# Second attention of an audio tower on Trainium2: order of the softmax weights, the rows' turns and the low halves within a chunk

## The reference

```python
Q = (x @ Wq).reshape(B, T, h, k)        # 16 heads of 32
K, V = x @ Wk, x @ Wv                   # 4 heads of 32, each shared by four of Q's
Q = Q * cos + rotate_half(Q) * sin      # and K in the same way
scores = where(causal, Q @ K.T / sqrt(k), -inf)
A = softmax(scores)                     # within a sequence of 23 tokens
h = h + (A @ V) @ Wo                    # x is the layer norm of h
```

## Time and profile before

| | us |
|---|---|
| Median of 3 runs | 1508.97 |
| Lowest, highest | 1508.01, 1509.94 |
| The profiled execution | 1494.19 |
| its span | 1492.4 |
| PE busy | 1298.2 |
| DVE busy | 916.2 |
| ACT busy | 630.0 |
| POOL busy | 259.8 |
| Second attention, first projection to last product with V | 1142.2 to 1290.1 |

### The profile page before, as it was taken

One profiled execution on the slowest core, in us unless ns is written; L12 is line 12 of the kernel. 1 busy time (PEld: TensorE's weight loads), 2 busy tenths in 40 slices (PEclk: granted clock), 3 DMA queues, 4 the chain that ended last, 5 costly groups with the idle time before them and its releaser, 6 DMA issues.

```text
span 1492.4 us, 30422 instructions
## 1 busy us (share of the span) xinstructions
PE 1298.2 (87%) x10676; PEld 831.1 (56%) x10690; DVE 916.2 (61%) x1918; ACT 630.0 (42%) x1066; POOL 259.8 (17%) x304
## 2 busy tenths in 40 slices
PE   6878899999999999995857999999996778668997
PEld 3446677777777777773523444444543556424443
DVE  5776365555566556558782454555347765688886
ACT  3444444344444434441413444444533332236664
POOL 2444000000000000000003232233338510020000
PEclk9996999999999999997678999999998778789999
DMA  5121343435334353421404777776436620000000
GB/s 183 59 76 43 101 170 139 179 133 183 126 142 169 141 182 128 184 85 43 172 1 167 260 261 240 276 260 229 133 115 149 90 33 2 2 0 8 22 21 32
DMA packets 42703, 184.26 MB, mean 123 GB/s; under 512 B 8688, under 2 KB 9200, under 8 KB 34832
## 3 DMA queue, kind: packets, MB, share of 16 engines
q0 software_dynamic: 19744, 95.41, 19.4%
q1 hardware_dynamic: 19440, 75.41, 14.5%
q10 hardware_dynamic: 3456, 12.58, 2.4%
HBM read 135.65 MB, written 47.73 MB: 123 GB/s over the span
## 4 chain that ended last, share of the span: by engine, by line
PE 56%; DVE 18%; issue 14%; POOL 4%; ACT 4%; DMA 2%; DVEq 1%; ACTq 0%; POOLq 0%; SPq 0%
PE ps L919 14%; PE ps L920 14%; PE ps L921 14%; PE ps L1026 3%; PE ps L1009 3%; DVE ff L1991 2%; DVE amf L1998 1%; PE ps L1110 1%; POOL wide L512 1%; POOL rt_out L472 1%; PE ps L1042 1%; PE ps L1249 1%; POOL h L518 1%; PE ps L1342 1%; PE ps L1360 1%
## 5 line engine op out<-in xcount | busy, mean ns | idle before, releaser
L919 PE MATMUL ps<-nT_hi,wa_hi 128*128 128x368 f16 x448 | 147.2, 329 | 11.9 <-DVE wa_lo L1389 8.1
L920 PE MATMUL ps<-nT_lo,wa_hi 128*128 128x368 f16 x448 | 146.9, 328 | 0.0
L921 PE MATMUL ps<-nT_hi,wa_lo 128*128 128x368 f16 x448 | 146.3, 327 | 0.0
L1553 DVE TENSOR_TENSOR a<-sq,E 92x368 f32<-92x368 f32 x64 | 31.7, 535 | 136.2 <-ACT sq L690 136.2
L1725 DVE SCALAR_TENSOR_TENSOR nrm<-ps,xg,nrm 128x256 f32<-128x256 f32 x61 | 29.5, 483 | 133.7 <-ACT nrm L733 116.4
L502 POOL DMA_INDIRECT xg<-xrow,idx x61 | 61.0, 1001 | 276.9 <-PE ps L1110 121.9
L920 PE MATMUL ps<-wa_lo,nT_hi 128*92 128x128 f16 (+1 forms) x560 | 107.6, 236 | 0.0
L919 PE MATMUL ps<-wa_hi,nT_hi 128*92 128x128 f16 (+1 forms) x560 | 107.6, 236 | 0.0
L921 PE MATMUL ps<-wa_hi,nT_lo 128*92 128x128 f16 (+1 forms) x560 | 107.2, 236 | 0.0
L919 PE MATMUL ps<-wide,xT 128*128 x244 | 93.7, 384 | 13.2 <-issue 10.1
L702 ACT ACTIVATE yT_hi<-ps 128x368 f16<-128x368 f32 x64 | 27.9, 475 | 164.5 <-PE ps L1042 164.5
(11 more groups left out here) (308 smaller groups left out, 3354.5 us busy)
## 6 DMA issues: line engine op xcount, KB each, us to landing
we_st<-in_we POOLq DMA_DIRECT2D x16, 1536.0 KB, 6.8
wsp<-we_sp POOLq DMA_DIRECT2D x16, 1536.0 KB, 5.3
wide<-wsp SPq DMA_DIRECT2D x16, 1536.0 KB, 7.5
yslot<-yt POOLq DMA_DIRECT2D x61, 256.0 KB, 4.2
wq_st<-in_ffq SPq DMA_DIRECT2D x24, 512.0 KB, 6.1
wq_st<-in_ffq ACTq DMA_DIRECT2D x24, 512.0 KB, 4.4
wide<-in_wa SPq DMA_DIRECT2D x10, 1024.0 KB, 4.8
xt<-in_x SPq DMA_DIRECT2D x12, 512.0 KB, 3.4
```

The costliest lines, as they stand in the source:

```text
L919: nc.tensor.matmul(dst, lhs[0], rhs[0], start=start, stop=False)
L920: nc.tensor.matmul(dst, lhs[0], rhs[1], start=False, stop=False)
L921: return nc.tensor.matmul(dst, lhs[1], rhs[0], start=False, stop=stop)
L1553: V.tensor_tensor(B["a"][0:AT, j], B["sq"][0:AT, j], B["E"][0:AT, 2 * j:2 * j + 2].unsqueeze(2).broadcast_to([AT, 2, REP, AT]), ALU.mult). ...
```

## The change

Four orders and two waits are changed, all in the second attention. No operation is added or removed.

- DVE: `weights(c - 1)` stands between the root's request and `group_shift` in place of behind it. The three low halves of an inner chunk stand together behind `rotated`. `y_low(c - 1)` no longer stands at the end of chunk c, but behind rotate 0 and 1 of chunk c + 1 (the last one behind the loop).
- PE: the turn of the softmax weights stands right behind V, and the turns of all three row tiles behind it. It now waits only for the low half of the last tile of the group before. Each turn of a row tile gets a wait for ACT's move of the quarter of the softmax weights that lay in its bank.
- ACT: projection 4 is moved ahead of the normed tiles, and the quarters of the softmax weights are moved before the high halves of the rows.

```diff
@@ ScalarE
                 moved(c, 2)
                 moved(c, 3)
+                moved(c, 4)
                 if inner:
                     normed(k)
                     normed(k + 1)
-                moved(c, 4)
+                moved(c, 5)
+                if c:
+                    weights_turned(c - 1)
                 if inner:
                     high(k)
                     normed(k + 2)
-                moved(c, 5)
-                if inner:
                     high(k + 1)
                     high(k + 2)
-                if c:
-                    weights_turned(c - 1)
-                else:
+                if c == 0:
...
@@ TensorE
-            def turn(c):
+            def turn(c, k):
                 pe.wait_ge(f_s, c + 1)
-                pe.wait_ge(ln_lo, ready(2 * NT + min(NT, GT * (c + 3)) - 1))
+                pe.wait_ge(ln_lo, ready(2 * NT + k))
...
                 for j in range(2, 6):
                     project(c, j)
-                    if inner and j == 4:
-                        row_turn_l1(k)
+                if c:
+                    turn(c - 1, k - 1)
                 if inner:
-                    row_turn_l1(k + 1)
-                    row_turn_l1(k + 2)
-                if c:
-                    turn(c - 1)
+                    for j in range(k, k + GT):
+                        pe.wait_ge(f_pe, ready(4 * (c - 1) + 2 + j % 2))
+                        row_turn_l1(j)
                 scores(c)
...
-            turn(CH - 1)
+            turn(CH - 1, NT - 1)
@@ VectorE
                 rotate(c, 0)
                 rotate(c, 1)
+                if c > 1:
+                    y_low(c - 2)
                 if c:
                     if c + 1 < CH:
                         group_stats(c + 1)
+                    weights(c - 1)
+                    if c + 1 < CH:
                         group_shift(c + 1)
-                    weights(c - 1)
                 for j in range(2, 5):
                     rotate(c, j)
-                    if 0 < c < CH - 1:
-                        low(k + j - 2)
                 rotated(c)
+                if 0 < c < CH - 1:
+                    for j in range(GT):
+                        low(k + j)
...
                     centred(c)
-                    y_low(c - 1)
+            y_low(CH - 2)
```

## The result

| | before | changed |
|---|---|---|
| Median | 1508.59 us (4 runs) | 1493.83 us (4 runs) |
| Lowest, highest | 1508.01, 1509.94 | 1492.69, 1496.49 |
| The profiled execution | 1494.19 | 1496.49 |
| its span | 1492.4 | 1494.7 |

The ratio is 0.9903, with an interval from 0.9886 to 0.9921: 14.8 us faster, where 6.8 were forecast. The two profiled executions say something else again: the changed kernel's took 2.3 us longer. Both facts have to be explained.

What follows compares the result with a forecast made beforehand. The prediction took a ring between PE and DVE, each idle once a chunk, as the bound. Chunk terms +0.6 - 3.5 - 3.9 = -6.8 us, off the median 1508.97, gave 1502.2 us, range 1495.5 to 1507.

Steps and rivals of the forecast that it cites:

- The baseline: Whole execution: 14.8 us between profiled 1494.19 and median 1508.97 lie outside the changed work; the gain comes off the median.
- Theory A: Follow-up runs' expectation: only the second attention got faster, about 8 us; the rest of 14.8 us is stalls elsewhere.
- sign of being wrong: Behind the second attention: the prediction is wrong if the stage is shortened and the feed-forward part grows.
- The new wait at the third row's turn: Inner chunks, PE: the turn waits about 2 us for the first low half, now behind `qp`, with scores queued behind.
- The loss of 0.6 us: Chunk 1: scores end at 1202.5 against 1201.8, with turn, masks and scores priced at the low clock; +0.6 us.
- -3.5 forecast: Chunk 2: rotates ahead of `y_low` start statistics 3.5 us sooner; scores at the low clock; gain 3.5 us.
- the root's wait: Chunks 1 and 2: softmax weights no longer stand behind the root's result; 1.1 us of the root saved in chunk 2.
- -3.9 forecast: Chunk 3: rotates fill the wait for `y_high`, `qp` 3.3 us earlier, scores 0.6 us cheaper; gain 3.9 us.
- the price of the scores: Chunk 3: scores cost 6.4 us, between 7.04 (gap of 4.02) and 5.73 (gap of 1.10).
- projection 4's earlier move on ACT: ACT: taken as free because ACT was idle; without it rotate 4 would be late by 1.52 us.
- Rival 1: Clock still high when scores of chunk 1 or 2 begin: 2.3 us a chunk, 1499.9 or 1497.6 us; chance 0.27.
- Rival 3: Clock stays low through V and turns of chunks 1 and 2: 17.8 us slower, 1520 us; chance 0.06.

Runs made afterwards that it cites:

- both additions: Changed kernel with the first low half ahead of kr and qp, plus repeated masks in all chunks; 1493.5 us (fourth set), 1479.2 us (sixth set).
- r1_after: Changed kernel run again without further edits, second set; 1489.2 us, ratio 0.9950 to the kernel before.
- r5_before: Kernel before, unchanged, run once more in the sixth set; 1499.0 us beside 1498.1.
- r1_ylow: Kernel before with only y_low moved behind rotate 0 and 1 of the next chunk, second set; 1488.1 us, ratio 0.9924.
- r4_warm: Changed kernel with masks repeated three times more ahead of the third row's turn in inner chunks, fifth set; 1482.8 us, ratio 0.9907.
- r5_combo: Changed kernel with first low half ahead of kr and qp and repeated masks in every chunk, sixth set; 1479.2 us, ratio 0.9898.

## Why the prediction was right or wrong

All traces of the stage, in us, by the same marks as above:

| trace | chunk 0 | chunk 1 | chunk 2 | chunk 3 | tail | stage |
|---|---|---|---|---|---|---|
| before, mean of 4 | 22.1 | 39.2 | 36.8 | 31.2 | 20.6 | 149.9 |
| changed, mean of 5 | 21.2 | 39.2 | 34.0 | 25.3 | 20.9 | 140.6 |
| difference | -0.9 | 0.0 | -2.8 | -5.9 | +0.2 | -9.3 |
| forecast | 0 | +0.6 | -3.5 | -3.9 | 0 | -6.8 |
| only y_low moved (2 traces) | 22.6, 21.0 | 41.9, 39.7 | 33.7, 32.6 | 28.5, 24.2 | 21.1, 20.6 | 147.8, 138.1 |
| all but y_low | 22.8 | 37.1 | 37.5 | 31.4 | 20.2 | 149.0 |
| masks repeated (2 traces) | 22.1, 22.4 | 35.9, 37.1 | 30.9, 31.2 | 25.2, 25.0 | 21.0, 21.1 | 135.1, 136.8 |

And the times of the two kernels in each set of executions, with the stalls that its traces have:

| set | before | changed | difference | ACT idle without a releaser |
|---|---|---|---|---|
| first (medians of the result) | 1508.6 | 1493.8 | 14.8 | changed 9.2; before's trace (1494.19) none |
| second | 1497.8 | 1489.2 | 8.6 | none in 4 traces |
| third | 1497.1 | 1489.5 | 7.6 | none in 3 |
| fourth | 1506.8 | 1495.9 | 10.9 | 16.5; 14.4; 6.8 and 7.9: in 3 traces |
| fifth | 1497.6 | 1489.0 | 8.6 | none in 4 |

**The baseline was the step that failed.** The prediction says that the 14.8 us between the profiled execution of 1494.19 us and the median of 1508.97 "lie outside the changed work", and takes a difference off the median as if they were a constant of both kernels. They are not one. The times come at two levels: sets at about 1507 for the kernel before have traces in which ACT stands idle for 6.8 to 16.5 us ahead of the second attention with no releaser; the 13 traces of the other sets (with the last one's, 1498.1 for the kernel before) and the first trace of before have none. The profiled execution of before belongs to the low level, its medians to the high one. About 11 of the 14.8 us are the distance of the levels (1508.6 and 1497.6), the rest is how far one execution lay below its level. At the low level the change was worth 7.6 to 8.6 us, near the forecast 6.8 and within a factor of 1.3. At the high level the two kernels differed by 10.9 and 14.8.

**Theory A holds in part.** The stage gains 7 to 9 us (8.0, 8.8 and 7.2 in the pairs of the first, second and fifth set, 9.3 between the means; it took 139.3 us in the changed trace of the fourth set), and the stall is not the change's doing. But the expectation that the stall is a matter of chance for each execution was wrong: it comes with the set. Why the kernel before loses 9 to 11 us to the high level and the changed one 4 to 7 **stays open**. It is no steady property of the old order either: between the second and the fourth set, the kernel with only `y_low` moved lost 13.6 us, and between the sixth and the fourth, the one with both additions lost 14.3. So the 10.9 and 14.8 us can't be called the worth of the change. No trace of the kernel before at the high level exists. That the stall shifts the stage in time, so that the clock changes at other pieces of work and more scores of the kernel before run low, is a thought that the traces neither show nor exclude.

**Behind the stage.** The prediction named as a sign of being wrong that the stage is shortened and the feed-forward part behind it grows. In the first pair it did, by 3.3 us. Over all traces this part takes 201.6 to 201.9 us or 203.9 to 205.0, in both kernels: the kernel before has the short one in two of four traces, the changed one in two of five. So the sign was met by chance as far as these traces tell; what sets the two lengths is not shown.

**Chunk 1: the wait was right, the way of the clock was not.** The new wait at the third row's turn was forecast at 2 us and measured at 2.81, 2.05, 2.87, 2.65 and 2.08; scores at 7.04 were forecast and measured in four of five traces. But the prediction argued that the clock would not rise ahead of the scores. In fact it stood at 2.4 GHz through V and the turn of the softmax weights and fell from there: in the wait in two traces, within the scores in one, and in the other two already in the row turns ahead of the wait, as here in r1_after (eight took 1.15 us in the first trace):

```profile
1191.28 1.97 PE L913 MATMUL ps<-ident,nrm 128*128 128x128 f32 x8 [0.20 <-ACT wide L792]
```

The loss of 0.6 us became 0.0 in the mean only because one of the four traces of before, r5_before, had 7.04 us for its scores, where the earlier trace rows had 4.14. Against the other three (mean 38.2 us) chunk 1 lost 1.0 us. Against the first trace alone it lost 2.0 us, since projections 0 and 1 ran at the low clock for longer too (`moved` of projection 1 waited 2.46 us in place of 1.39).

**Chunk 2: right, a little too large.** -3.5 forecast, -2.8 measured; 33.9 us from end to end, where 32.5 to 33.5 was said. All that was named is there: rotates ahead of `y_low`, the root's wait gone, V without a wait, scores at 7.04.

**Chunk 3: mechanism right, term mis-sized.** -3.9 forecast, -5.9 measured. `qp` came earlier by about what was said and the wait shrank to between 1.30 and 1.84 us. The step at fault is the price of the scores, which the prediction put between 7.04 us (gap of 4.02) and 5.73 (gap of 1.10), at 6.4: they cost 4.1 to 4.2 us in all five traces. I had set the price by the length of the gap alone, and that doesn't order the traces: in r1_ylow a gap of 1.93 us stands ahead of 6.96 us. The clock stood at 2.4 GHz through turns, masks and gap in the kernel before as well. What differs is when it fell: in the four traces of before it fell ahead of the scores or within their first 0.7 us (6.5 to 7.04 us), in the five of the changed kernel only some 3.2 us into them. Rows of before (turns and masks, then scores, with the clock as third number from the end) and of r1_ylow:

```profile
1255.40:1258.80 3.40, 2.84 (x20) 1.00 0.00 0
1262.40:1269.60 7.20, 7.02 (x128) 0.50 0.01 2
1262.89 6.96 PE L1249 MATMUL ps<-kr,qp 32*128 32x23 f32 x128 [1.93 <-DVE qp L1858]
```

The term was too high by 2.2 us, more than the whole miss.

**Chunk 0** has no change and was 1.3 us shorter in the first pair, 0.9 in the mean: again the clock during its scores (4.17 in place of 5.73). They took 5.4 to 6.5 us in the traces of before and 3.8 to 5.8 in those of the changed kernel; nothing in the change explains that, and it is left as chance.

**The new order by itself** brings nothing that can be told (0.9987 to 1.0024), as its expectation of 0.999 to 1.000 said. Whether projection 4's earlier move on ACT is free, as the prediction took it, was not tried apart.

**Rivals.** Rival 1 (clock high in the scores of chunks 1 and 2) did not happen in the changed kernel beyond the first half microsecond of one trace, but it is real: with the hole filled, 6.2 and 7.7 us are gained, where the prediction had 2.3 a chunk and 7.8 at best. Rival 3 did not occur. Its price was also added up too low: V takes 2.8 us at the high level, and by the ratio of the projections (3.0 to 1.6) it would take 2.4 us more at the low one, not 1.9. The range had room for the clock's luck within the changed kernel, but none for that of the kernel before, or for the level of a set; 1495.5 to 1507 was drawn around a centre that took the high level over unchanged.

**The rule on transposes** that the prediction quotes (the Trainium skill, TensorE: Matmul & The Clock Gate, Part 4: PE-mode transpose) is against the traces here as well: from 1193.6 to 1197.4 us PE did nothing but sixteen transposes of softmax weights and eight of rows, at 2.4 GHz (PEclk 1.00 in the stretch from 1193.0 to 1198.0), and eight took 1.09 to 1.15 us, where r1_after has 1.97 with the low clock. The clock was high before they began, so this shows that they run at the full rate, not that they raise it.

## What to carry to other kernels

Before a forecast is taken off a median, put the profiled execution beside the median and ask where the gap is. Executions of one kernel in one set differed here by 2 to 15 us, so a gap of a few microseconds can be chance; a profiled execution that lay 14 us below every timed one was of another level. A row that stands for "before" can be one case of two as well, so a term that rests on one clock state deserves both prices on both sides. Where a stretch of small matmuls follows a hole of 2 to 3 us, repeating harmless full-size matmuls in the hole can pay: here 6.2 and 7.7 us over two chunks for work that is thrown away.

## What the runs showed of the hardware

- The 128 score matmuls of 32 rows cost 3.8 us when the granted clock was 1.00 throughout (r4_warm and r5_combo, chunk 2) and 7.04 us when it was 0.50 throughout. With a change on the way they cost something between: in chunk 1 of before it fell about 3.2 us into them (4.14), in chunk 2 of before it rose 0.6 us into them (4.02).
- The length of the idle time ahead of them did not tell what they cost: in chunk 3 it was 4.12 us behind a gap of 1.57 us (r1_after), 4.17 behind 1.84 (the first trace of the changed kernel), and 6.96 behind 1.93 (r1_ylow).
- Repeated masks (12 matmuls of 368 columns, 2.03 us at the high level) in a hole of 2.1 to 2.9 us shortened the stage by 5.4 and 5.1 us in the two pairs of traces.
- ACT stood idle for 6.8 to 16.5 us with no releaser in the profile, near the same place in all three traces of the fourth set, and in none of the third set on the same chip. What it waits for isn't shown.
- What follows the stage, which no kernel here changes, took 201.6 to 201.9 us in some traced executions and 203.9 to 205.0 in the others.
